# Windowed-attention kernel: loading the postponed half rows one row at a time, spread over regions

## The chip, the cores and the metric

The kernel runs on one core of one Trainium2 chip. The metric is the device time of one execution in microseconds. The median of three runs of the kernel before is 1763.54 us. All data are float32.

## What is computed

An image batch x of shape 8 x 56 x 56 x 256 goes through group normalization (32 groups) and a bi-level routing attention, and the result is added to x:

```python
q, k, v = split(conv1x1(groupnorm(x)))             # 256 channels each
a_r = mean_per_region(q) @ mean_per_region(k)      # 7 x 7 = 49 regions of 8 x 8 pixels
idx = top_k(a_r, 4)                                # each region takes the keys and values of 4 regions
o = softmax(q * 256**-0.5 @ k[idx]) @ v[idx]       # 8 heads of 32
out = x + conv1x1_out(o + depthwise3x3(v))         # the 3x3 part is called lepe
```

The four regions that a region attends to are known only at run time. So keys are gathered by GpSimd from SBUF, and values by DMA from DRAM.

## The kernel before, in words

**Tiling.** A "row" is one of the 56 rows of regions in the batch (7 per image): 8 pixel rows of 56 pixels, 448 positions, held as two channel halves of 128 partitions. One row of both halves is 448 KB, one half 224 KB. A region r is one of 392; row g holds regions 7g to 7g+6.

**Order of work.** Every engine has a hand-written instruction stream, a loop over steps s (0 to 56) and in it over the seven regions rc. In the turn of region r = 7s + rc, TensorE turns the first half of the softmax probabilities of r, computes the scores of r+1 (`scores`, L1098), attends region r-1 (`attend`, L1125), turns the other half, and does a slice of the projections. ScalarE does the exponentials and empties PSUM banks, VectorE the maxima, the scaling and the 3x3 taps (L737). There are three slots of gathered values, v_sel.

**SyncE's queue.** `select_values` (L322) issues four DMAs of 64 KB for each region, 256 KB in all, each for one of the chosen regions. In the turn of r it does so for r+2, once the slot is free, that is once region r-1 has been attended. `attend` waits for all four. This queue also stores the values of new rows (`store_values`, L301).

**GpSimd's queue.** In the turn of r it gathers the keys for r+2 (`gather_keys`, L382, waits for the scores of r), adds the attention output of r-2 to the lepe row (`take_region`, L393), and then does what the turn has by its number: `mid_tap` in 1 and 2, `halo` in 3 or 6, `normalize` in 4 and 5, the residual load `load_resid` (L449, L451) in 5, the store of the previous row `store_row` (L456, L459) in 6. It runs about a region ahead of TensorE, since its waits are for earlier regions. Its DMAs have a queue of their own; an issue holds the engine for over half a microsecond.

**Postponed rows.** For 25 rows (`LATE`) the second half (output channels 128 to 255) of the output projection isn't done in the row's own step. Instead, `spill_row` (L463) writes the finished lepe row to DRAM, and the last steps, from TAIL = 49 on, do the projection, since nothing else is left to project there. `LATE_GROUPS` are nine groups of two or three rows; `LATE_AT` gives group 0 to step 49, 1 to 50 and so on to 4 at step 53, then groups 5 and 6 (five rows) to step 54, and 7 and 8 (five rows) to step 55. `late_rows(s)` is the list of the step's rows. TensorE projects the first three in turns 0, 1 and 2 of the step (`project_late`, L1038), the fourth and fifth in turns 5 and 6; VectorE then adds bias and x (`late_half`, L835).

Their inputs come through GpSimd's queue. `load_late` (L477) brings a group of spilled rows into slots of xn: two DMAs (one per channel half) of 672 KB for three rows, 448 KB for two. It is called in turn 4 of the step before for each group of the step. It waits until the rows' slots are free (for the first three groups, until the q projections of the rows there before are done; later, until the group three before has been projected), and until all 25 spills have landed. `load_late_x` (L485) brings the second half of x for a group in one DMA (672 or 448 KB), in turn 6 of the step before, into the space of k_all that is no longer used. It waits until the last even image's keys have been gathered, or until the store of the group three before is done. `store_late` (L490) stores a group in one DMA, in turn 3 of its own step, the second group of a step in turn 1 of the next. There are three sets of three slots; each set has one semaphore for the rows and one for x.

```python
LATE_GROUPS = ((5, 12, 19), (26, 33, 40), (6, 13, 20), (27, 34, 41), (8, 15, 22), (29, 36, 43), (10, 17),
               (24, 31, 38), (45, 47))
LATE_AT = {TAIL: (0,), TAIL + 1: (1,), TAIL + 2: (2,), TAIL + 3: (3,), TAIL + 4: (4,), TAIL + 5: (5, 6),
           TAIL + 6: (7, 8)}
```

Of the kernel before, what the change touches and what calls it, by code (L numbers as in the profile page):

```python
# [20 lines left out]
KC = C // P  # L21
# [17 lines left out]
X_RING = 2 * NWIN  # L39
# [4 lines left out]
ROWS = NB * NWIN  # L44
# [11 lines left out]
LATE = [g for group in LATE_GROUPS for g in group]  # L56
LATE_AT = {TAIL: (0,), TAIL + 1: (1,), TAIL + 2: (2,), TAIL + 3: (3,), TAIL + 4: (4,), TAIL + 5: (5, 6),
           TAIL + 6: (7, 8)}
LATE_SETS = 3
LATE_SLOTS = 3  # L60
# [22 lines left out]
def late_rows(s):  # L83
    return [g for i in LATE_AT.get(s, ()) for g in LATE_GROUPS[i]]
# [51 lines left out]
def attention_kernel(nc, x, w_qkv, w_out, b_qkv, b_out, w_tap, b_tap, ident_d, group_d, v_dram, spill, out):  # L136
    place, early_chunks = chunk_places()

    with ExitStack() as ctx:
# [3 lines left out]
        def sem(name):  # L143
            return ctx.enter_context(nc.semaphore(name))
# [58 lines left out]
        resid_in = [sem(f"resid_in{i}") for i in range(2)]  # L203
        out_stored = [sem(f"out_stored{i}") for i in range(2)]
        spilled = sem("spilled")
        late_in = [sem(f"late_in{i}") for i in range(LATE_SETS)]
        late_x_in = [sem(f"late_x_in{i}") for i in range(LATE_SETS)]
        late_stored = [sem(f"late_stored{i}") for i in range(LATE_SETS)]

        chunk_full = [sem(f"chunk_full{i}") for i in range(EARLY_BANKS)]  # L210
# [24 lines left out]
        def late_set(i):  # L235
            first = LATE_SLOTS * (i % LATE_SETS)
            return slice(first, first + len(LATE_GROUPS[i]))

        def late_place(g):
            i = next(i for i, group in enumerate(LATE_GROUPS) if g in group)  # L240
            return i, LATE_SLOTS * (i % LATE_SETS) + LATE_GROUPS[i].index(g)

        def late_dram(rows, i):
            group = LATE_GROUPS[i]
            return rows[group[0]:group[-1] + 1:group[1] - group[0], :, 1, :].rearrange("i p r -> p i r")
# [9 lines left out]
        def wait_full(eng, kind, n, k):  # L255
            i, before = place[kind, n, k]
            eng.wait_ge(chunk_full[i], before + 1)
# [109 lines left out]
        def _(pool):  # L367
# [94 lines left out]
                pool.wait_ge(o_row_done, NWIN * (g + 1))  # L462
                pool.dma_start(spill[LATE.index(g)], lepe[:, :, g % LEPE_RING, :]).then_inc(spilled, 16)  # L463

            def load_late(i):
                group = LATE_GROUPS[i]
                if i < LATE_SETS:
                    for j in range(len(group)):
                        wait_full(pool, "q", ROWS - X_RING + LATE_SLOTS * i + j, 0)
                        wait_full(pool, "q", ROWS - X_RING + LATE_SLOTS * i + j, 1)  # L470
                else:
                    for g in LATE_GROUPS[i - LATE_SETS]:
                        wait_full(pool, "late", g, 1)
                pool.wait_ge(spilled, 16 * len(LATE))
                at = LATE.index(group[0])
                for k in range(KC):
                    pool.dma_start(xn[:, k, late_set(i), :], spill[at:at + len(group), :, k, :].rearrange(  # L477
                        "i p r -> p i r")).then_inc(late_in[i % LATE_SETS], 16)

            def load_late_x(i):  # L480
                if i < LATE_SETS:
                    pool.wait_ge(k_sel_done, NREG * (NB - 1))
                else:
                    pool.wait_ge(late_stored[i % LATE_SETS], 16 * (i // LATE_SETS))
                pool.dma_start(late_x[:, late_set(i), :], late_dram(x, i)).then_inc(late_x_in[i % LATE_SETS], 16)  # L485

            def store_late(i):
                for g in LATE_GROUPS[i]:
# [22 lines left out]
            for s in range(STEPS):  # L511
                rr, kv, xr = s % NWIN, s + KV_LEAD, s + STAT_LEAD
                for rc in range(NWIN):
                    r = s * NWIN + rc
                    if is_region(r + 2):
                        gather_keys(r + 2)
                    if is_region(r - 2):
                        take_region(r - 2)

                    if rc == 0 and is_row(s + LOAD_LEAD):  # L520
                        load_x(s + LOAD_LEAD)
                    elif rc == 1 and is_row(s + MID_LEAD):
                        mid_tap(s + MID_LEAD, 0)
                    elif rc == 2:
                        if is_row(s + MID_LEAD):
                            mid_tap(s + MID_LEAD, 1)
                        if s - 1 in LATE:
                            spill_row(s - 1)
                    elif rc == 3:
                        if rr == LAST and is_row(xr):  # L530
                            image_rstd(xr // NWIN)
                        if rr and is_row(kv):
                            halo(kv)
                    elif rc == 4 and is_row(s + NORM_LEAD):
                        normalize(s + NORM_LEAD, 1)
                    elif rc == 5:
                        if is_row(s + NORM_LEAD):
                            normalize(s + NORM_LEAD, 0)
                        if is_row(s):
                            load_resid(s)  # L540
                    elif rc == 6:
                        if is_row(s - 1):
                            store_row(s - 1)
                        if rr == 0 and is_row(kv):
                            halo(kv)

                    if rc == 1:
                        for i in LATE_AT.get(s - 1, ())[1:]:
                            store_late(i)
                    elif rc == 3:  # L550
                        for i in LATE_AT.get(s, ())[:1]:
                            store_late(i)
                    elif rc == 4:
                        for i in LATE_AT.get(s + 1, ()):
                            load_late(i)
                    elif rc == 6:
                        for i in LATE_AT.get(s + 1, ()):
                            load_late_x(i)

        @block.scalar  # L560
        def _(act):
# [150 lines left out]
        def _(dve):  # L712
# [117 lines left out]

            def late_half(g):
                i, j = late_place(g)
                dve.wait_ge(late_x_in[i % LATE_SETS], 16 * (i // LATE_SETS + 1))
                wait_full(dve, "late", g, 1)
                dve.scalar_tensor_tensor(late_x[:, j, :], bank_of("late", g, 1)[:, 0:ROW], bout[:, 1:2],  # L835
                                         late_x[:, j, :], ALU.add, ALU.add).then_inc(free("late", g, 1), 1)
# [158 lines left out]
        def _(pe):  # L995
# [34 lines left out]
            def project_late(g, first, last):  # L1030
                place_i, slot = late_place(g)
                for i in range(first, last):
                    half, part = divmod(i, KC)
                    cols = slice(HALF * half, HALF * (half + 1))
                    if i == 0:
                        pe.wait_ge(late_in[place_i % LATE_SETS], 16 * KC * (place_i // LATE_SETS + 1))
                        wait_bank(pe, "late", g, 1)
                    ins = pe.matmul(bank_of("late", g, 1)[:, cols], wout[:, part, P:2 * P], xn[:, part, slot, cols],  # L1038
                                    start=(part == 0), stop=(part == KC - 1))
                if last == QUARTERS:  # L1040
                    ins.then_inc(full("late", g, 1), 1)
# [301 lines left out]
```

## Time and profile before

| | |
|---|---|
| median of 3 runs | 1763.54 us (1760.93 to 1764.39) |
| the profiled execution's own time | 1764.58 us |
| its span, first to last instruction | 1762.8 us |
| granted TensorE clock, mean | 0.993 |
| TensorE busy | 1697.1 us (96%) |
| VectorE busy | 1527.3 us (87%) |
| ScalarE busy | 1463.7 us (83%) |
| GpSimd busy | 1151.4 us (65%) |
| SyncE's DMA queue | 129.71 MB |
| GpSimd's DMA queue | 100.02 MB |

How to read the rows: times are microseconds of one execution, from the start of the span. PE is TensorE's matmuls, PEld its weight loads, DVE VectorE, ACT ScalarE, POOL GpSimd, SP SyncE. Granted clock 1.00 is 2.4 GHz, 0.50 is 1.2 GHz. DMA share is the mean busy share of the core's 16 DMA engines; it can be a little over 1 in a short window. The tail, from which most rows are taken, lasts from about 1541 us to the end.

### The profile page before, as it was taken

The numbers are of one execution on the slowest core, as the hardware profiler recorded it, in microseconds if no ns is written. First come the engines' busy times: TensorE is split into PE (matmuls) and PEld (weight loads), VectorE is DVE, ScalarE is ACT, GpSimd is POOL, SyncE is SP. The second block draws the span as 40 slices with busy tenths as digits, with TensorE's granted clock in tenths as the row PEclk, the third lists the DMA queues.
The fourth block names the chain that finished last, engine by engine and source line by source line (L and its number), as shares of the span: only waits on it lengthen the run. The fifth ranks groups of instructions, "written<-read, shape, count | busy, mean of one in ns | idle before, by whom it ended". The sixth has DMA issues, their size and how long they took to land.

```text
span 1762.8 us, 76270 instructions
## 1 busy us (share of the span) xinstructions
PE 1697.1 (96%) x26568; PEld 1371.2 (78%) x26568; DVE 1527.3 (87%) x3329; ACT 1463.7 (83%) x4793; POOL 1151.4 (65%) x2525
## 2 busy tenths in 40 slices
PE   4999999999999999999999999999999999999987
PEld 4878887877778778778778778787787787777765
DVE  6478989899898899988898989988998888899984
ACT  1488888888888888888888888888888888878764
POOL 3256666677666776776766776667666666666762
PEclk9999999999999999999999999999999999999998
DMA  5323434343434443444443444434433333556563
GB/s 186 90 83 111 146 108 142 111 145 118 133 121 128 123 142 119 128 127 125 126 133 120 134 129 118 134 117 134 131 119 109 114 107 113 156 176 222 174 235 136
DMA packets 163945, 234.61 MB, mean 133 GB/s; under 512 B 18864, under 2 KB 146240, under 8 KB 163568
## 3 DMA queue, kind: packets, MB, share of 16 engines
q1 hardware_dynamic: 141408, 129.71, 25.1%
q0 software_dynamic: 22160, 100.02, 17.0%
q8 instruction: 219, 3.59, 0.9%
q14 instruction: 158, 1.29, 0.2%
HBM read 166.80 MB, written 62.85 MB: 130 GB/s over the span
## 4 chain that ended last, share of the span: by engine, by line
PE 64%; ACT 17%; DVE 11%; issue 4%; DMA 3%; POOL 0%; SPq 0%; POOLq 0%; ACTq 0%; DVEq 0%
PE chunk_bank L1011 18%; ACT probs L617 14%; PE pt_bank L1111 13%; PE s_bank L1098 12%; PE o_bank L1125 8%; DVE neg_max L840 6%; PE chunk_bank L1025 6%; DVE lepe L737 3%; PE chunk_bank L1053 2%; DMA v_sel<-v_dram 2%; ACT probs_t L624 2%; PE o_bank L1135 1%; PE s_bank L1011 1%; ACT v_stage L589 1%; PE chunk_bank L1073 1%
## 5 line engine op out<-in xcount | busy, mean ns | idle before, releaser
L617 ACT ACTIVATE probs<-s_bank,neg_max 128x256 f32<-128x256 f32 x1568 | 739.4, 484 | 158.3 <-DVE neg_max L840 157.7
L840 DVE TENSOR_REDUCE neg_max<-s_bank 128x2 f32<-128x512 f32 x784 | 506.1, 686 | 134.5 <-PE s_bank L1098 133.2
L737 DVE SCALAR_TENSOR_TENSOR lepe<-v_band,taps,lepe 128x448 f32<-128x448 f32 x896 | 611.1, 728 | 0.0
L382 POOL COPY k_sel<-k_all 128x128 f32 x1568 | 408.9, 305 | 290.9 <-PE s_bank L1098 277.2
L1011 PE MATMUL chunk_bank<-xn,wqkv 128*128 128x224 f32 x2544 | 570.6, 356 | 2.5 <-DVE xn L773 2.5
L624 ACT COPY probs_t<-pt_bank 128x512 f32<-128x512 f32 x784 | 467.3, 596 | 69.9 <-PE pt_bank L1111 68.9
L1111 PE MATMUL pt_bank<-ident,probs 128*128 128x128 f32 x3136 | 494.0, 280 | 0.2
L1011 PEld LDWEIGHTS chunk_bank<-xn,wqkv 128*128 128x128 f32 x2544 | 442.4, 192 | 9.3 <-DVE xn L773 2.6
L1111 PEld LDWEIGHTS pt_bank<-ident,probs 128*128 128x128 f32 x3136 | 359.7, 141 | 53.4 <-ACT probs_t L624 0.9
L393 POOL TENSOR_TENSOR lepe<-o_norm,lepe 128x128 f32<-128x128 f32 x392 | 251.2, 641 | 165.5 <-DVE o_norm L858 164.2
L617 ACT ACTIVATION_READ_ACCUMULATOR probs<-s_bank,neg_max 128x1 f32 x1568 | 332.2, 212 | 0.0
L1125 PEld LDWEIGHTS o_bank<-probs_t,v_sel 128*32 128x32 f32 x12544 | 193.8, 110 | 160.3 <-issue 149.0
L1098 PE MATMUL s_bank<-k_sel,q_all 32*64 32x256 f32 x6272 | 270.6, 400 | 18.9 <-ACT probs L617 6.9
L1125 PE MATMUL o_bank<-probs_t,v_sel 128*32 128x64 f32 x12544 | 257.4, 222 | 9.3 <-DMA v_sel<-v_dram 8.5
L1098 PEld LDWEIGHTS s_bank<-k_sel,q_all 32*64 32x64 f32 x6272 | 92.0, 130 | 93.6 <-ACT probs L617 57.3
L404 POOL TENSOR_SCALAR lepe<-v_band,taps,btap 128x448 f32<-128x448 f32 x112 | 162.2, 1448 | 0.0
L1025 PE MATMUL chunk_bank<-lepe,wout 128*128 128x224 f32 x696 | 151.0, 353 | 1.0 <-POOL lepe L393 1.0
L442 POOL TENSOR_SCALAR xn<-xn,rstd,shift 128x448 f32<-128x448 f32 x96 | 123.1, 1282 | 12.3 <-DVE shift_sum L801 12.3
L1025 PEld LDWEIGHTS chunk_bank<-lepe,wout 128*128 128x128 f32 x696 | 123.5, 190 | 2.3 <-POOL lepe L393 1.2
L851 DVE COPY recips<-rdenom 128x128 f32<-128x128 f32 x392 | 108.5, 277 | 13.4
L858 DVE TENSOR_TENSOR o_norm<-o_bank,recips_t 128x128 f32<-128x128 f32 x392 | 110.1, 281 | 6.7 <-PE o_bank L1125 6.7
L628 ACT COPY recips_t<-o_bank 128x128 f32<-128x128 f32 x392 | 113.9, 291 | 0.7 <-PE o_bank L1135 0.7
(77 smaller groups left out, 1299.5 us busy)
## 6 DMA issues: line engine op xcount, KB each, us to landing
v_sel<-v_dram SPq DMA_DIRECT2D x1568, 64.0 KB
xn<-x_dram POOLq DMA_DIRECT2D x56, 448.0 KB, 5.0
v_dram<-v_stage SPq DMA_DIRECT2D x112, 224.0 KB
resid<-x_dram POOLq DMA_DIRECT2D x31, 448.0 KB, 4.2
out_dram<-resid POOLq DMA_DIRECT2D x31, 448.0 KB
spill<-lepe POOLq DMA_DIRECT2D x25, 448.0 KB, 3.6
xn<-spill POOLq DMA_DIRECT2D x14, 672.0 KB, 6.7
resid<-x_dram POOLq DMA_DIRECT2D x25, 224.0 KB, 3.4
```

Source lines behind the costliest of these rows:

```text
L382: last = pool.tensor_copy(k_sel[:, r % K_SLOTS, :, RT * j:RT * (j + 1)], k_all[:, b % 2, :, bass.ds(reg[j] * RT, RT)])
L393: pool.tensor_tensor(cells, o_norm[:, r % 2, :].rearrange("p (k r c) -> p k r c", k=KC, r=RS), cells, ALU.add).then_inc(o_row_done, 1)
L404: pool.tensor_scalar(in_image(lepe[:, k, n % LEPE_RING, :]), v_band[:, n % BANDS, k, 1:1 + RS, 1:1 + W], taps[:, k, MID_TAP:MID_TAP + 1], ...
L617: act.activation(probs[:, u, :], s_bank[:, u, 0:KEYS], ACT.Exp, bias=neg_max[:, r % 2, u:u + 1], accum_out=denom[:, r % 2, u:u + 1]).then_ ...
L624: act.copy(probs_t[:, r % 2, hf, :], pt_bank[:, :]).then_inc(probs_t_evac, 1)
L737: ins = dve.scalar_tensor_tensor(row, v_band[:, n % BANDS, k, t // 3:t // 3 + RS, t % 3:t % 3 + W], taps[:, k, t:t + 1], row, ALU.mult, AL ...
L840: dve.tensor_reduce(neg_max[:, r % 2, 2 * hf:2 * hf + 2], s_bank[:, 2 * hf:2 * hf + 2, 0:KEYS], AX.X, ALU.max, negate=True).then_inc(max_d ...
L1011: ins = pe.matmul(bank_of(kind, n, k)[:, cols], wqkv[:, part, col:col + P], xn[:, part, n % X_RING, cols], start=(part == 0), stop=(part = ...
L1025: ins = pe.matmul(bank_of("out", g, m)[:, cols], wout[:, part, P * m:P * (m + 1)], lepe[:, part, g % LEPE_RING, cols], start=(part == 0), ...
L1098: last = pe.matmul(s_bank[RT * k:RT * (k + 1), u, 0:KEYS], q_all[s, g % Q_RING, k, rc, :], k_sel[s, r % K_SLOTS, k, :], start=True, stop=True)
L1111: t = pe.transpose(pt_bank[:, at:at + P], probs[:, u, P * c:P * (c + 1)], ident[:])
L1125: last = pe.matmul(o_bank[HD * u:HD * (u + 1), RT * k:RT * (k + 1)], v_sel[:, r % V_SLOTS, c, HD * head:HD * (head + 1)], probs_t[:, r % 2 ...
```

## The change

The two loading functions now take a row g in place of a group i, and each slot has its own semaphore for rows and for x, nine of each in place of three. `load_late(g)` issues one DMA of 448 KB for both channel halves; it waits only for its own slot, or for the group three before as until now, and only for the spills up to its own row. `load_late_x(g)` issues one DMA of 224 KB. In the step before, the first three rows are loaded in turns 3, 4 and 5, one each, and their x in turn 6. Where a step has five rows (54 and 55), the fourth and fifth are loaded in turns 0 and 1 of the step itself, each with its x right behind it. The stores of groups stay as they are. The rest is the waits of the readers, `late_half` and `project_late`.

```diff
--- before.py
+++ after.py
@@ -203,8 +203,8 @@
         resid_in = [sem(f"resid_in{i}") for i in range(2)]
         out_stored = [sem(f"out_stored{i}") for i in range(2)]
         spilled = sem("spilled")
-        late_in = [sem(f"late_in{i}") for i in range(LATE_SETS)]
-        late_x_in = [sem(f"late_x_in{i}") for i in range(LATE_SETS)]
+        late_in = [sem(f"late_in{i}") for i in range(LATE_SETS * LATE_SLOTS)]
+        late_x_in = [sem(f"late_x_in{i}") for i in range(LATE_SETS * LATE_SLOTS)]
         late_stored = [sem(f"late_stored{i}") for i in range(LATE_SETS)]
 
         chunk_full = [sem(f"chunk_full{i}") for i in range(EARLY_BANKS)]
@@ -462,27 +462,24 @@
                 pool.wait_ge(o_row_done, NWIN * (g + 1))
                 pool.dma_start(spill[LATE.index(g)], lepe[:, :, g % LEPE_RING, :]).then_inc(spilled, 16)
 
-            def load_late(i):
-                group = LATE_GROUPS[i]
+            def load_late(g):
+                i, slot = late_place(g)
                 if i < LATE_SETS:
-                    for j in range(len(group)):
-                        wait_full(pool, "q", ROWS - X_RING + LATE_SLOTS * i + j, 0)
-                        wait_full(pool, "q", ROWS - X_RING + LATE_SLOTS * i + j, 1)
+                    wait_full(pool, "q", ROWS - X_RING + slot, 0)
+                    wait_full(pool, "q", ROWS - X_RING + slot, 1)
                 else:
-                    for g in LATE_GROUPS[i - LATE_SETS]:
-                        wait_full(pool, "late", g, 1)
-                pool.wait_ge(spilled, 16 * len(LATE))
-                at = LATE.index(group[0])
-                for k in range(KC):
-                    pool.dma_start(xn[:, k, late_set(i), :], spill[at:at + len(group), :, k, :].rearrange(
-                        "i p r -> p i r")).then_inc(late_in[i % LATE_SETS], 16)
-
-            def load_late_x(i):
+                    for before in LATE_GROUPS[i - LATE_SETS]:
+                        wait_full(pool, "late", before, 1)
+                pool.wait_ge(spilled, 16 * (sorted(LATE).index(g) + 1))
+                pool.dma_start(xn[:, :, slot, :], spill[LATE.index(g)]).then_inc(late_in[slot], 16)
+
+            def load_late_x(g):
+                i, slot = late_place(g)
                 if i < LATE_SETS:
                     pool.wait_ge(k_sel_done, NREG * (NB - 1))
                 else:
                     pool.wait_ge(late_stored[i % LATE_SETS], 16 * (i // LATE_SETS))
-                pool.dma_start(late_x[:, late_set(i), :], late_dram(x, i)).then_inc(late_x_in[i % LATE_SETS], 16)
+                pool.dma_start(late_x[:, slot, :], x[g, :, 1, :]).then_inc(late_x_in[slot], 16)
 
             def store_late(i):
                 for g in LATE_GROUPS[i]:
@@ -550,12 +547,15 @@
                     elif rc == 3:
                         for i in LATE_AT.get(s, ())[:1]:
                             store_late(i)
-                    elif rc == 4:
-                        for i in LATE_AT.get(s + 1, ()):
-                            load_late(i)
+
+                    if rc >= 3 and late_rows(s + 1)[rc - 3:rc - 2] and rc < 6:
+                        load_late(late_rows(s + 1)[rc - 3])
                     elif rc == 6:
-                        for i in LATE_AT.get(s + 1, ()):
-                            load_late_x(i)
+                        for g in late_rows(s + 1)[:3]:
+                            load_late_x(g)
+                    elif rc < 2 and late_rows(s)[rc + 3:rc + 4]:
+                        load_late(late_rows(s)[rc + 3])
+                        load_late_x(late_rows(s)[rc + 3])
 
         @block.scalar
         def _(act):
@@ -830,7 +830,7 @@
 
             def late_half(g):
                 i, j = late_place(g)
-                dve.wait_ge(late_x_in[i % LATE_SETS], 16 * (i // LATE_SETS + 1))
+                dve.wait_ge(late_x_in[j], 16 * (i // LATE_SETS + 1))
                 wait_full(dve, "late", g, 1)
                 dve.scalar_tensor_tensor(late_x[:, j, :], bank_of("late", g, 1)[:, 0:ROW], bout[:, 1:2],
                                          late_x[:, j, :], ALU.add, ALU.add).then_inc(free("late", g, 1), 1)
@@ -1033,7 +1033,7 @@
                     half, part = divmod(i, KC)
                     cols = slice(HALF * half, HALF * (half + 1))
                     if i == 0:
-                        pe.wait_ge(late_in[place_i % LATE_SETS], 16 * KC * (place_i // LATE_SETS + 1))
+                        pe.wait_ge(late_in[slot], 16 * (place_i // LATE_SETS + 1))
                         wait_bank(pe, "late", g, 1)
                     ins = pe.matmul(bank_of("late", g, 1)[:, cols], wout[:, part, P:2 * P], xn[:, part, slot, cols],
                                     start=(part == 0), stop=(part == KC - 1))
```

## Rows read from the trace of the kernel before

**Rows 1.** The page, busy tenths in 40 slices of the span.
```profile
PE   4999999999999999999999999999999999999987
...
DMA  5323434343434443444443444434433333556563
```

**Rows 2.** Windows, L1098 alone: length, busy (x instructions), PEclk, DMA share, GB/s.
```profile
1545.00:1550.30 5.30, 0.69 (x16) 0.24 (x16) 1.00 0.39 125
1550.30:1683.50 133.20, 22.81 (x528) 7.81 (x528) 1.00 0.63 203
1683.50:1694.30 10.80, 0.69 (x16) 0.24 (x16) 0.68 0.55 196
1694.30:1718.70 24.40, 4.14 (x96) 1.42 (x96) 1.00 0.63 207
1718.70:1728.20 9.50, 0.69 (x16) 0.24 (x16) 0.64 0.69 248
1728.20:1744.20 16.00, 2.76 (x64) 0.94 (x64) 1.00 0.32 102
```

**Rows 3.** Timeline of weight loads: start, us, instructions, [idle before <- its end].
```profile
1546.57 0.49 PEld L1125 LDWEIGHTS o_bank<-probs_t,v_sel 128*32 128x32 f32 x32 [1.28 <-DMA v_sel<-v_dram]
...
1683.59 0.24 PEld L1098 LDWEIGHTS s_bank<-k_sel,q_all 32*64 32x64 f32 x16 [0.30 <-ACT probs L617]
1688.58 0.84 PEld L1125 LDWEIGHTS o_bank<-probs_t,v_sel 128*32 128x32 f32 x32 [4.75 <-DMA v_sel<-v_dram]
...
1694.38 0.23 PEld L1098 LDWEIGHTS s_bank<-k_sel,q_all 32*64 32x64 f32 x16 [0.17 <-issue]
...
1722.20 0.84 PEld L1125 LDWEIGHTS o_bank<-probs_t,v_sel 128*32 128x32 f32 x32 [3.20 <-DMA v_sel<-v_dram]
```

**Rows 4.** All instructions that read v_sel, whole span: waits (us, times).
```profile
  PEld o_bank L1125: 10.7, 5
```

**Rows 5.** The chain that ended last, 1676 to 1700: start, us, what.
```profile
1675.69 12.85 DMA v_sel<-v_dram
```

**Rows 6.** Timeline of POOL, steps 48 and 53.
```profile
1540.14 1.72 POOL L382 COPY k_sel<-k_all 128x128 f32 x4
...
1671.72 2.98 POOL L477 DMA_DIRECT2D xn<-spill  x4
...
1676.35 0.57 POOL L451 DMA_DIRECT2D resid<-x_dram  x1
...
1678.74 0.58 POOL L459 DMA_DIRECT2D out_dram<-resid  x1
1679.31 1.49 POOL L485 DMA_DIRECT2D k_all<-x_dram  x2
1680.80 0.99 POOL L382 COPY k_sel<-k_all 128x128 f32 x4
```

**Rows 7.** Windows, all engines: PE, PEld, DVE, ACT, POOL, PEclk, DMA share, GB/s.
```profile
1671.00:1687.00 16.00, 13.02 (x216) 9.65 (x214) 14.17 (x30) 12.49 (x45) 12.56 (x28) 1.00 0.92 317
1679.00:1683.00 4.00, 3.93 (x67) 3.04 (x66) 3.79 (x9) 3.60 (x15) 3.62 (x8) 1.00 1.05 356
1691.00:1695.00 4.00, 4.00 (x29) 2.98 (x28) 1.43 (x4) 2.03 (x7) 0.00 (x0) 0.62 0.25 77
```

**Rows 8.** DMA issues (KB, us to landing), then lines (duration ns min/median/max).
```profile
resid<-x_dram POOLq DMA_DIRECT2D x31, 448.0 KB, 4.2
...
xn<-spill POOLq DMA_DIRECT2D x14, 672.0 KB, 6.7
resid<-x_dram POOLq DMA_DIRECT2D x25, 224.0 KB, 3.4
...
L449 POOL DMA_DIRECT2D resid<-x_dram x25: 596/596/651, 264.1 to 1503.7; - x25
...
L463 POOL DMA_DIRECT2D spill<-lepe x25: 673/693/711, 280.3 to 1520.6; - x25
...
L477 POOL DMA_DIRECT2D xn<-spill x18: 724/767/798, 1527.8 to 1708.6; - x18
```

## The prediction, on record before the changed kernel ran

> **What bounds the kernel now.** I read four things in this order: the page's slices, the length of one region in the last part, the wait that ends late there, and what moved on the DMA engines meanwhile.
>
> The slices [rows 1] show TensorE at 9 tenths almost everywhere, so over most of the span the kernel is paced by the PE queue, which the change doesn't touch. What stands out is the end: the DMA row rises from 3 or 4 tenths to 5 and 6 in the last eight slices.
>
> Every region issues one group of 16 score matmuls (L1098), so counting them measures the pace [rows 2]. A region of the tail takes 4.00 us (64 matmuls in 16.0 us). From 1550.3 to 1683.5 there are 528, 33 regions in 133.2 us, which is 1.2 us over 33 x 4.00. But one region takes 10.8 us and another 9.5 us, at a mean granted clock of 0.68 and 0.64. They cost 6.8 and 5.5 us over 4.0, **12.3 us together**.
>
> Inside the first one [rows 3]: scores at 1683.59, then nothing until the attend matmuls (L1125) start at 1688.58, after 4.75 us of idle ended by the DMA into v_sel. From there the 32 weight loads take 0.84 us where they took 0.49 at 1546.57: behind the idle time TensorE runs at its 1.2 GHz level instead of 2.4 GHz, and the next scores come at 1694.38. The second region has 3.20 us of idle at 1722.20 and the same 0.84 us behind it. So each stall costs about twice its idle time in the first case (4.75 becomes 6.8) and 3.2 becomes 5.5 in the second. Over the whole execution the weight loads waited for v_sel five times, 10.7 us, and all five lie in the tail [rows 4]. There is also 1.3 us in a region of step 49 (5.3 us from 1545.0 to 1550.3 with 16 score matmuls [rows 2]), with a 1.28 us wait for v_sel in it [rows 3].
>
> Why v_sel is late: the chain of waits names one 64 KB transfer that was issued at 1675.69 and took 12.85 us [rows 5]. It was wanted at about 1684.0, 8.3 us after issue. Just before and after its issue POOL had put into its queue [rows 6] four loads of spilled rows (2240 KB, region 4 of step 53), a residual row (448 KB), a store (448 KB) and two loads of x for late rows (1120 KB). With 256 KB of values per region for four regions that is 5280 KB. The 16 us from 1671 to 1687 moved 317 GB/s, 5.07 MB or some 4950 KB, at a share around 1 in the middle [rows 7]. So the DMA engines were saturated by that burst, and the value gathers stood beside it. At 1718.7 the burst for step 55 does it again.
>
> **The change, part by part.** The bytes stay the same. For steps with three late rows, two loads of 672 KB at region 4 become three of 448 KB at regions 3, 4 and 5. For the two steps with five late rows (54 and 55), four loads at region 4 become three there and two in regions 0 and 1 of the step itself. The late x loads go from one of 672 KB at region 6 to three of 224 KB at region 6, and in the five-row steps the last two x rows follow their rows to regions 0 and 1.
>
> *Backlog.* I take 356 GB/s [rows 7] as what the engines can do: about 1390 KB in a 4.0 us region. Demand before for step 54, region 3 of step 53 onward (values 256 KB each; the residual row in region 5, the two stores in 3 and 6): 928, 2496, 704, 1824, 256, 256, 256 KB. After: 1376, 704, 1152, 1376, 928, 928, 256 KB. No region is above capacity, while before region 4 alone exceeded it by 1100 KB and region 6 again by 430. For a second comparison take three consecutive regions: after, the heaviest (5, 6, 0) hold 3456 KB; a three-row step before held 1600 + 704 + 1376 = 3680 KB in regions 4 to 6, and such steps ran with 1.2 us lost in 33 regions [rows 2]. So the five-row steps should now behave like three-row ones. I take both long stalls as gone: **-12.3 us**, idle and slow clock together, since the clock fell only behind the idle time.
>
> *Step 49.* Its 1.3 us comes from the burst of 1344 KB at region 4 of step 48. After, 896 KB are issued by then and 448 KB later, so the value stores and the first gather of the new image land earlier, but the later load joins the x loads. Bounds: 0 and 1.3 recovered; I take -0.7.
>
> *The small remainders.* 1.2 us in the 33 regions [rows 2] and 0.4 in the six between the stalls. The 0.4 is a region with three taps and a late row on VectorE, and stays. Of the 1.2 I take half, -0.5; bounds 0 and -1.2.
>
> *Issues on POOL.* Before, 18 loads and 9 x loads; after, 25 and 25. An issue of 448 KB holds POOL 0.69 us, one of 224 KB 0.60, the present ones 0.77 [rows 8] and 0.75 [rows 6]: 32.2 - 20.6 = 11.6 us more of POOL, in about 230 us. What hides it: key gathers (L382) for region r+2 wait only for the scores of r and are used two scores later. In the burst of step 53 the gather behind the two x loads ran from 1680.80 to 1681.79 [rows 6]; its scores would have come at 1687.6, one unstalled region after 1683.59 [rows 3], so it was 5.8 us early. At most three issues are added in one stretch (one at region 5, two at region 6), 2.1 us, and the slack is over 5. Without that cover each microsecond would land on scores: 11.6 us at most. In the first step of an image, 49, the gathers were already catching up: the third ended at 1541.86 [rows 6] for scores at 1545.0, 3.2 us of slack. I take 0; bounds 0 and +3. The queue of SP gets no new instruction.
>
> *Waits.* load_late drops the wait for all 25 spills (now only those up to its own row) and the waits for a whole group. Later positions reach buffers that were freed at least three regions before (the fourth and fifth rows of step 55 follow the late rows of step 54's regions 0 to 2 and their store at region 3). The rows have at least three regions, 12 us, between issue and use, against landings of 6.7 us with 672 KB [rows 8]. No new stall there: 0. The x rows now land one by one, so the first late row of a step isn't held for three. That is in the -0.7 above.
>
> Sum: -12.3 - 0.7 - 0.5 = **-13.5 us**. The profiled execution took 1764.58 us around a span of 1762.8; it would take 1751.1. The median of the three runs is 1763.54, 1.0 below it, so I predict **1750.0 us**.
>
> **The rivals.** (a) *One collision remains.* The x loads at region 6, the stores and the two displaced rows follow one another closely through regions 5 to 1, and a gather there meets them. For it: 1376 KB in region 6 is at capacity. Against it: the three-row comparison. It would keep about one stall of 5.5 to 6.8: some 1757 us.
>
> (b) *Nothing is gained*, because what delays the gathers is the total in the tail and not the burst, or the released load is only moved to the next regions. Then 1763.5. Against it: windows like 1691 to 1695, with a DMA share of 0.25 [rows 7], right behind the saturated ones, so there is room to move into. The Trainium skill (DMA: Bandwidth & Descriptors, Queues, rings and completion order) says each DMA engine goes round the queues it has work for, one packet at a time; by that rule a deep POOL queue could hold SP's small gathers back only by a share and not by its whole depth. The 12.85 us of a 64 KB transfer [rows 5] shows that the share is poor when the other queue stays full.
>
> (c) *Slower: the fixed cost of each transfer decides.* From 224 KB in 3.4 us and 448 KB in 4.2 us [rows 8], a transfer has 2.6 us that don't depend on size. If POOL's queue served its transfers one after the other, steps 54 and 55 would have four more each (10 for 6): 10.4 us per step in the queue that is already full, 20.8 in all, of which the idle DMA windows of a step might cover half. The stalls would stay and grow by 10.4: 1774 us. It decides once the fixed parts of a step's transfers no longer overlap. Against it: four loads issued within 3 us, with what followed, moved at 356 GB/s [rows 6, 7]. The Trainium skill (DMA: Bandwidth & Descriptors, Bandwidth) has a rule that speaks against the change: batch to 1 MiB or more, for transfers below it stay short of peak; its fit gives 2.0 us of fixed cost. No row here shows that cost serially.
>
> **How the numbers follow.** The forecast 0.74, (a) 0.13, (b) 0.07, (c) and anything like it on POOL 0.06. The range starts at 1747 (all 15.2 us of excess recovered gives 1748.3, and one run of before was 2.6 under the median) and goes to 1759, which takes in +3 for POOL and case (a). Less than 0.2% (3.5 us) can't be told from no change here. Faster 0.87, same 0.07, slower 0.06.
>
> **What would show it.** Right: no wait of L1125 for v_sel over 1 us after 1541; every region in 1683 to 1730 near 4.0 us at clock 1.00; no 4 us window at share 1 twice in a row in the tail; L382 still waiting for scores, with no score matmul behind POOL. Wrong: a 1.30 us group of weight loads anywhere in the tail, a region over 6 us, or L1098 waiting for L382.

## The result, and the profile after

| | before | changed |
|---|---|---|
| median, first series | 1763.34 us (4 runs) | 1753.09 us (4 runs, 1751.71 to 1755.16) |
| ratio | | 0.9946, 95% interval 0.9933 to 0.9959 |
| profiled execution | 1764.58 us | 1755.16 us |
| span | 1762.8 us | 1753.4 us |
| granted clock, mean | 0.993 | 0.996 |

The change made the kernel 10.3 us faster. A second series of six runs gave 1752.51 us against 1764.13, ratio 0.9942 (0.9925 to 0.996). One execution each of e7 and e10 below took 2741 and 2740 us, at a mean granted clock of 0.62 and 0.56, and their medians and all ratios leave it out. The forecast of 1750.0 is 3.1 us below the first median, inside the range.

Three traces are read below with one yardstick: the time from the 50th last group of scores (L1098) to the last, 49 intervals, the last image. The scores of consecutive regions lie 3.99 or 4.00 us apart where nothing stands in the way, which makes 196. The kernel before took **211.2 us** for it, the changed one **200.9** in its first profile and **197.4** in a second one (e12 below). The image before it took 206.2 in the kernel before and 206.1 and 206.2 in the other two.

In the 40 slices of the page, beside [rows 1], the DMA row ends in 34466574 tenths, where it ended in 33556563: about as high as before, for the bytes haven't changed. Windows of the changed kernel with L1098 alone, as in [rows 2] (length, PE busy and count, PEld busy and count, clock, DMA share, GB/s):

```profile
1547.90:1683.80 135.90, 23.51 (x544) 8.05 (x544) 1.00 0.65 206
1683.80:1691.30 7.50, 0.69 (x16) 0.24 (x16) 0.77 0.62 197
1691.30:1716.90 25.60, 4.14 (x96) 1.42 (x96) 1.00 0.70 223
1716.90:1732.90 16.00, 2.77 (x64) 0.95 (x64) 1.00 0.60 198
```

34 regions in 135.9 us: the losses ahead of step 54 are gone. Of the two long regions one is left, 7.5 us at a mean clock of 0.77, in step 54; the one of step 55 is gone. The six regions behind it took 25.6 us, 1.6 over 24: two of them 4.4 us each, and one, in turn 4 of step 54, 4.8 us. In that one two 3x3 taps on VectorE took 2.56 us, where the next pair took 1.47:

```profile
1697.57 2.56 DVE L737 SCALAR_TENSOR_TENSOR lepe<-v_band,taps,lepe 128x448 f32<-128x448 f32 x2
1702.38 1.47 DVE L737 SCALAR_TENSOR_TENSOR lepe<-v_band,taps,lepe 128x448 f32<-128x448 f32 x2
```

The timeline of the weight loads (start, us; idle before), beside [rows 3]:

```profile
1683.85 0.24 PEld L1098 LDWEIGHTS s_bank<-k_sel,q_all 32*64 32x64 f32 x16 [0.30 <-ACT probs L617]
1686.54 0.83 PEld L1125 LDWEIGHTS o_bank<-probs_t,v_sel 128*32 128x32 f32 x32 [2.44 <-DMA v_sel<-v_dram]
1691.38 0.23 PEld L1098 LDWEIGHTS s_bank<-k_sel,q_all 32*64 32x64 f32 x16 [0.17 <-issue]
```

It is the same kind of stall as before, 2.44 us of idle in place of 4.75, and again the lower clock level behind it: 0.83 us for 32 weight loads that take 0.49. The transfer it waited for, from the chain of waits, beside [rows 5]:

```profile
1677.43 9.06 DMA v_sel<-v_dram
```

9.06 us in place of 12.85. And all that reads v_sel, beside [rows 4] (us of waiting, times):

```profile
  PEld o_bank L1125: 2.8, 2
```

GpSimd's issues, beside [rows 8] (count, duration in ns min/median/max):

```profile
L474 POOL DMA_DIRECT2D xn<-spill x25: 704/724/753, 1523.4 to 1716.6; - x25
...
L482 POOL DMA_DIRECT2D k_all<-x_dram x25: 537/539/567, 1538.0 to 1717.4; - x25
```

That is 31.6 us of issues where there were 20.5. No score matmul in the tail waited for a key gather. The waits of GpSimd's gathers and of the scores' weight loads, 1500 to 1753 (us, times, longest):

```profile
POOL k_sel L382 <- PE s_bank L1098: 30.9, 26, 5.4
PEld s_bank L1098 <- ACT probs L617: 15.9, 52, 0.4
```

**Where the values stood.** The view that I hadn't split by queue in the prediction is the one that explains most. For each 4.0 us window, the packets, MB and share of the 16 engines of GpSimd's queue (q0) and SyncE's queue (q1), which in this stretch carries the value gathers. They need 0.26 MB a region. The kernel before, 1675.7 to 1679.7:

```profile
q0 software_dynamic: 312, 1.44, 97.1%
q1 hardware_dynamic: 62, 0.06, 4.8%
```

and 1679.7 to 1683.7:

```profile
q0 software_dynamic: 259, 1.25, 89.4%
q1 hardware_dynamic: 141, 0.13, 10.2%
```

The changed kernel, 1673.6 to 1677.6:

```profile
q0 software_dynamic: 227, 1.15, 82.1%
q1 hardware_dynamic: 182, 0.16, 13.3%
```

and 1677.6 to 1681.6:

```profile
q0 software_dynamic: 249, 0.98, 72.7%
q1 hardware_dynamic: 214, 0.20, 15.6%
```

So the values can fall behind while the engines move less than the 356 GB/s that the prediction took as their capacity: the two windows after hold 1.31 and 1.18 MB, against 1.42, and the two queues together 95% and 88% of the engines' time. In these four windows SyncE's queue got less than it needs: 0.06 and 0.13 MB before, 0.16 and 0.20 after. After, it is still short, only less so. But the shortfall alone doesn't tell whether a stall comes. In the four windows from the start of the burst this execution has 0.11, 0.30, 0.16 and 0.20 MB, and e12, the same kernel without the stall, has 0.10, 0.30, 0.20 and 0.15.

### The profile page after: what moved, and what is told of

Its sections match the earlier page's. It is cut to its first block, busy times and chain, and to the rows that moved or that the text cites. A ratio compares the mean times of both kernels' runs of the same rounds, so it can differ in the third digit from the quotient of the medians.

```text
span 1753.4 us, 76313 instructions
## 1 busy us (share of the span) xinstructions
PE 1692.8 (97%) x26568; PEld 1368.0 (78%) x26568; DVE 1524.4 (87%) x3329; ACT 1460.4 (83%) x4793; POOL 1155.3 (66%) x2548
## 4 chain that ended last, share of the span: by engine, by line
PE 64%; ACT 18%; DVE 12%; issue 4%; DMA 1%; SPq 0%; POOL 0%; POOLq 0%; ACTq 0%; DVEq 0%
PE chunk_bank L1011 17%; ACT probs L617 14%; PE pt_bank L1111 13%; PE s_bank L1098 13%; PE o_bank L1125 8%; DVE neg_max L840 6%; PE chunk_bank L1025 6%; DVE lepe L737 4%; PE chunk_bank L1053 2%; ACT probs_t L624 2%; PE o_bank L1135 1%; PE s_bank L1011 1%; ACT v_stage L589 1%; PE chunk_bank L1073 1%; ACT q_all L598 1%
## 5 line engine op out<-in xcount | busy, mean ns | idle before, releaser
L1098 PE MATMUL s_bank<-k_sel,q_all 32*64 32x256 f32 x6272 | 270.6, 400 | 18.3 <-ACT probs L617 4.5
L1098 PEld LDWEIGHTS s_bank<-k_sel,q_all 32*64 32x64 f32 x6272 | 92.0, 130 | 93.1 <-ACT probs L617 57.1
L442 POOL TENSOR_SCALAR xn<-xn,rstd,shift 128x448 f32<-128x448 f32 x96 | 122.1, 1272 | 12.3 <-DVE shift_sum L801 12.3
L1135 PE MATMUL o_bank<-ident,recips 128*128 128x128 f32 x392 | 108.2, 276 | 4.6 <-DVE o_norm L858 3.6
```

The costliest lines, as they stand in the source:

```text
L1098: last = pe.matmul(s_bank[RT * k:RT * (k + 1), u, 0:KEYS], q_all[s, g % Q_RING, k, rc, :], k_sel[s, r % K_SLOTS, k, :], start=True, stop=True)
```

## The experiments

All are variants of the changed kernel unless said. "Last image" is the yardstick above (49 intervals; the expectation of e9 calls them 48 regions), in the variant's one profile; "waits" are those of the attend weight loads for v_sel in that execution. The intervals reach some 3 us to either side, so apart from e10 the medians don't tell the variants from each other, and one profile isn't enough either: the changed kernel itself read 200.9 and 197.4. In the diffs `...` marks lines left out.

| run | median us | ratio to before (95%) | last image us | waits for v_sel us, times |
|---|---|---|---|---|
| changed, first | 1753.09 | 0.9946 (0.9933 to 0.9959) | 200.9 | 2.8, 2 |
| e1 rows, one turn | 1756.74 | 0.9961 (0.9944 to 0.9979) | 202.2 | 7.2, 5 |
| e2 only five-row steps | 1752.39 | 0.9933 (0.9912 to 0.9954) | 199.4 | 0.8, 2 |
| e3 groups, spread | 1753.96 | 0.9946 (0.9925 to 0.9968) | 198.6 | 3.0, 4 |
| e4 rows in halves | 1752.43 | 0.9935 (0.9915 to 0.9956) | 198.7 | 0.6, 1 |
| e5 displaced later | 1753.53 | 0.9939 (0.9919 to 0.9958) | 197.5 | 1.6, 2 |
| e6 register load split | 1754.48 | 0.9943 (0.9924 to 0.9963) | 202.8 | 5.4, 6 |
| e7 both | 1753.89 | 0.9943 (0.9928 to 0.9957) | 201.9 | 3.8, 2 |
| e8 four rows not loaded | 1750.81 | 0.9924 (0.9902 to 0.9945) | 197.4 | 0.8, 1 |
| e9 halves, one turn | 1754.24 | 0.9949 (0.993 to 0.9969) | 201.4 | 3.4, 3 |
| e10 x by row alone | 1764.25 | 0.9999 (0.9986 to 1.0013) | 211.1 | 10.7, 6 |
| e11 later, in halves | 1752.37 | 0.9939 (0.9923 to 0.9956) | 198.4 | 0.8, 2 |
| e12 changed, again | 1752.51 | 0.9942 (0.9925 to 0.996) | 197.4 | 2.5, 4 |

**e1: the same transfers, at the old moments.**

```diff
-                    if rc >= 3 and late_rows(s + 1)[rc - 3:rc - 2] and rc < 6:
-                        load_late(late_rows(s + 1)[rc - 3])
+                    if rc == 4:
+                        for g in late_rows(s + 1):
+                            load_late(g)
...
-                        for g in late_rows(s + 1)[:3]:
+                        for g in late_rows(s + 1):
                             load_late_x(g)
-                    elif rc < 2 and late_rows(s)[rc + 3:rc + 4]:
-                        load_late(late_rows(s)[rc + 3])
-                        load_late_x(late_rows(s)[rc + 3])
```

> The same 25 and 25 transfers as the changed kernel, but all rows of a step are issued in turn 4 of the step before and all x in turn 6, as the groups were. Theory A, that the moments of the loads decide: the two long stalls of the kernel before return, and the time is 1762 to 1766 us. Theory B, that the size of a transfer decides (single rows mix better with the value gathers than groups of three): it stays at 1751 to 1755 us. Theory C, that each transfer has a serial fixed cost or that its issue on GpSimd shows: it is slower than the kernel before, above 1768 us.

Neither of the first two. 1756.7 us: 7.5 us below the kernel before (3.7 to 9.9 by the ratio's interval), so more than half of the gain is there, as the medians have it, although nothing is spread. The two stalls are still at steps 54 and 55, with 2.40 and 2.33 us of idle (before: 4.75 and 3.20), and the clock didn't fall behind them. Weight loads of e1, the first of the two:

```profile
1683.88 0.49 PEld L1123 LDWEIGHTS o_bank<-probs_t,v_sel 128*32 128x32 f32 x32 [2.40 <-DMA v_sel<-v_dram]
1687.11 0.23 PEld L1096 LDWEIGHTS s_bank<-k_sel,q_all 32*64 32x64 f32 x16 [0.17 <-issue]
```

So this stall costs 1.9 us where one with 2.44 us of idle and the lower clock cost the changed kernel 3.5. Theory C is out: 23 more transfers, with ten in place of six in the bursts for steps 54 and 55, made nothing slower. The edit changes more than the size: a row's transfer takes both channel halves of one row, where a group's took one half of two or three rows.

**e2: spreading only for the two five-row steps.**

```diff
-                    if rc >= 3 and late_rows(s + 1)[rc - 3:rc - 2] and rc < 6:
+                    if s + 1 < TAIL + 5:
+                        if rc == 4:
+                            for g in late_rows(s + 1):
+                                load_late(g)
+                    elif rc >= 3 and late_rows(s + 1)[rc - 3:rc - 2] and rc < 6:
...
-                    elif rc == 6:
+                    if rc == 6:
```

> Rows for steps 49 to 53 are issued in turn 4 all at once, those for steps 54 and 55 as in the changed kernel. If the gain comes from the two five-row steps alone: 1753 to 1756 us, with at most 1.5 us more than the changed kernel, in the regions behind the bursts of steps 48 to 52. If spreading the three-row steps is worth something of its own: above 1756.

1752.4 us: as good as the changed kernel. In its profile 2.1 us are lost in four single regions of steps 49 to 52, where e12 lost 0.8. What spreading the three-row steps is worth can't be told from nothing here; the gain that shows is in the steps with five rows.

**e3: the kernel before, with its groups at spread moments.**

```diff
-                    elif rc == 4:
-                        for i in LATE_AT.get(s + 1, ()):
-                            load_late(i)
-                    elif rc == 6:
-                        for i in LATE_AT.get(s + 1, ()):
-                            load_late_x(i)
+                    if rc in (3, 5):
+                        for i in LATE_AT.get(s + 1, ())[:1]:
+                            load_late(i, (rc - 3) // 2)
+                    elif rc == 6:
+                        for i in LATE_AT.get(s + 1, ())[:1]:
+                            load_late_x(i)
+                    elif rc < 2:
+                        for i in LATE_AT.get(s, ())[1:]:
+                            load_late(i, rc)
+                            if rc:
+                                load_late_x(i)
...
```

`load_late` takes the channel half as its second argument and issues that one alone; the first three groups wait for 24 of the 25 spills.

> The transfers of the kernel before (18 loads of groups and 9 of x) at spread moments: the two channel halves of the first group in turns 3 and 5, those of the second group of steps 54 and 55 in turns 0 and 1 of the step itself, with its x in turn 1. Theory A (moments): 1751 to 1756 us, like the changed kernel. Theory B (size of the transfer): 1760 to 1765 us, like the one before.

1754.0 us, last image 198.6: theory A. With e1 this gives the main finding: **either half of the change, the moments or the single rows, brings most of the gain alone**, and the two don't add up. For the single rows that is 7.5 us of 10.3, with intervals of e1 and the changed kernel that overlap.

**e4: twice as many transfers of rows.**

```diff
-                pool.dma_start(xn[:, :, slot, :], spill[LATE.index(g)]).then_inc(late_in[slot], 16)
+                for k in range(KC):
+                    pool.dma_start(xn[:, k, slot, :], spill[LATE.index(g), :, k, :]).then_inc(late_in[slot], 16)
...
```

TensorE's wait for a row counts both transfers.

> The changed kernel with each row load made as two transfers of 224 KB: 25 transfers and some 15 us of GpSimd's issue time more, the same bytes at the same moments. Theory A, issues and fixed costs hidden: within 1.5 us of the changed kernel, 1752 to 1755 us. Theory C, fixed cost of a transfer (2.6 us) or its issue time shows: 3 to 15 us slower than the changed kernel, with score matmuls that wait for the key gathers or a longer wait for v_sel.

Theory A again: 1752.4 us. GpSimd now issues for 40.5 us (27.2 + 13.3), 20 more than in the kernel before, and the median shows no time for it. Its profile isn't free of a trace of it, though: three regions took 4.45, 4.45 and 4.80 us, and beside them a pair of taps on VectorE took 2.20, 2.20 and 2.55 us, while GpSimd was issuing and copying keys. No pair took so long in the last image of the kernel before or of e1 and e9, which issue at the old moments. Whether GpSimd's work at these moments slows the taps wasn't tested.

**e5: the fourth and fifth rows in turns 1 and 2.**

```diff
-                    elif rc < 2 and late_rows(s)[rc + 3:rc + 4]:
-                        load_late(late_rows(s)[rc + 3])
-                        load_late_x(late_rows(s)[rc + 3])
+                    elif 1 <= rc < 3 and late_rows(s)[rc + 2:rc + 3]:
+                        load_late(late_rows(s)[rc + 2])
+                        load_late_x(late_rows(s)[rc + 2])
```

> The changed kernel with the fourth and fifth rows of steps 54 and 55 (and their x) loaded in turns 1 and 2 instead of 0 and 1. Its one remaining stall is at the attend of the step's first region in turn 1 of step 54 (2.44 us idle, 3.5 us in all), while the displaced loads of turns 0 and 1 are under way. If those loads hold the values back: the stall is gone or under 1 us and the time is 2 to 4 us below the changed kernel. If it is the short lead of that region's gathers (behind SyncE's register load of 2.2 us) with the transfers of turns 5 and 6: the stall stays at 2 us or more and the time is within 1 us.

No stall in its profile, last image 197.5, but the median is that of the changed kernel. What I took for a cure was chance: e12 shows the unedited kernel without the stall too, and e7 has these moments and the stall.

**e6: SyncE reads its region numbers in three portions.**

```diff
 GROUPS = {0: NWIN}
+SP_GROUPS = {0: 2, 2: 3, 5: 2}
...
-                if r % NWIN in GROUPS:
-                    value_regions.update(chosen(mybir.EngineType.SP, r, GROUPS[r % NWIN]))
+                if r % NWIN in SP_GROUPS:
+                    value_regions.update(chosen(mybir.EngineType.SP, r, SP_GROUPS[r % NWIN]))
```

> The changed kernel with SyncE's register load of 28 region numbers per step (2.2 us, right ahead of the gathers for the step's first region) split into three of 8, 12 and 8. If the short lead of that region's gathers makes the remaining stall: they are issued 1 us or more earlier, the stall of 2.44 us shrinks by as much, and the time falls by 1 to 3 us. If the load of the DMA engines alone makes it: no shift of the stall, time within 1 us, or slightly slower by the additional register loads.

No gain, 1754.5. The stall came in this profile too, with 2.72 us of idle, and the transfer at its end took 10.05 us. It had been issued 7.4 us before it was wanted, in the changed kernel 6.7 us before, so the lead grew by 0.7 us and the stall didn't shrink. A portion isn't cheap: the load of 8 or 12 numbers took 1.07 us, the one of all 28 took 2.17 (medians of 14 and of 4 of SyncE's register loads from 1600 us on, in e6 and in the changed kernel).

**e7: e5 and e6 together** (both diffs).

> Both of the above together. If each takes away its own part, there is no wait for v_sel over 0.5 us in the tail and the time is 1748 to 1751 us: the changed kernel less 3.5 us. If one is the whole cause, this is the same as that one alone.

It missed: 1753.9 us, with a wait of 3.17 us one region ahead of that place, in a region of 8.3 us. Neither edit takes the stall away for certain.

**e8: the fourth and fifth rows aren't loaded.** It bounds what moving them can give.

```diff
-                    elif rc < 2 and late_rows(s)[rc + 3:rc + 4]:
-                        load_late(late_rows(s)[rc + 3])
-                        load_late_x(late_rows(s)[rc + 3])
...
```

The waits for these four rows and their x are left out too, so their part of the output is not computed from the right data.

> The changed kernel without the loads of the fourth and fifth rows of steps 54 and 55 at all (rows 10, 17, 45 and 47; their second output half is computed from what lies in the slots), so 2688 KB less. It bounds what any other moment for these loads can give: if they make the remaining stall, it is gone, 1749 to 1751 us; if the stall stays at 2 us or more, it is made by the rest, the loads of turns 5 and 6 and the short lead.

1750.8 us, as the first case said: at most some 2 us are left in the moments of these four rows. There is no stall in its profile, but e12 has none either, with the four rows loaded.

**e9: transfers of 224 KB, all at the old moments** (the diffs of e1 and e4).

> Every row of a step in turn 4 of the step before and every x in turn 6, as in the kernel before, but with transfers of 224 KB throughout (two for each row). The row-by-row kernel at these moments had two stalls with 2.40 and 2.33 us of idle where groups of 672 KB had 4.75 and 3.20. If the size of the transfers sets how long the value gathers are held up: less than 1.5 us of idle at each place, the last image's 48 regions in 197.5 to 200.5 us (202.2 with 448 KB, 211.2 with 672 KB), the time 1752 to 1755. If what was gained there came from something else than size: the stalls stay at 2 us and the time is 1756 or more.

Between the cases: 1754.2 us, idle for v_sel 1.16 us at step 55 and none at step 54, but the last image took 201.4, above what I gave, with losses of 1.6 us in a region of step 54 and 1.3 in one of step 49 among others. The 1.6 us came another way: VectorE waited for the x of a late row, whose transfer, issued at 1679.29, took 6.93 us, and the exponentials and TensorE waited behind it.

```profile
1686.24 0.68 DVE L834 SCALAR_TENSOR_TENSOR k_all<-chunk_bank,bout,k_all 128x448 f32<-128x448 f32 x1 [1.54 <-DMA k_all<-x_dram]
```

What SyncE's queue got, region by region from the start of the burst (first four windows of 4.0 us): 0.26, 0.06, 0.13, 0.12 MB in the kernel before; 0.21, 0.10, 0.14, 0.14 in e10 (below), with the rows still in groups; 0.22, 0.10, 0.15, 0.16 in e1 with single rows; 0.22, 0.15, 0.21, 0.26 here. Only e9 stands out clearly, and it isn't a matter of size alone: its ten issues of rows hold GpSimd for 5.35 us, where the four before took 2.98, and its x loads begin 11.0 us after the first row's, 7.6 in the kernel before and 8.6 in e1.

**e10: the kernel before with only the x loads by row.**

```diff
-                pool.dma_start(late_x[:, late_set(i), :], late_dram(x, i)).then_inc(late_x_in[i % LATE_SETS], 16)
+                for g in LATE_GROUPS[i]:
+                    slot = late_place(g)[1]
+                    pool.dma_start(late_x[:, slot, :], x[g, :, 1, :]).then_inc(late_x_in[slot], 16)
...
```

> The kernel before with only the x loads made row by row (224 KB instead of 672 or 448 KB), still all in turn 6; the spilled rows stay in groups in turn 4. If the x loads, the last to be queued ahead of the late gathers, hold them up by their size: a good part of the two long stalls goes, 1756 to 1760 us. If the large transfers of spilled rows do it, within 2 us of the kernel before.

Nothing: 1764.3, last image 211.1, waits of 3.45 and 3.79 us at the two places. The size of the x loads isn't what holds the values back. e1 differs from this mainly in the loads of spilled rows, which come first in the burst, so the gain of e1 is put down to them.

**e11: e4 and e5 together, the candidate for something better.**

> The changed kernel with both edits that left no stall in their profiles: displaced rows in turns 1 and 2, and each row in two transfers of 224 KB. The last image should take 197.5 to 199 us with no wait for v_sel over 1.3 us; the time 1751 to 1753.5 us. Since each edit alone gave 1752.4 and 1753.5, I expect no clear gain over the changed kernel: at most 2 us.

1752.4 us, as expected no measurable gain over the changed kernel.

**e12: the changed kernel once more.**

> The changed kernel once more, unedited, to see whether the stall of its first profile (2.44 us idle at the first region of step 54, 3.5 us in all) is in every execution. If it is: last image 200.5 to 201.5 us, 1752 to 1755 us. If it comes and goes: last image near 198 us.

It comes and goes. Its windows with L1098 alone:

```profile
1549.50:1705.30 155.80, 26.96 (x624) 9.23 (x624) 1.00 0.66 208
1705.30:1714.10 8.80, 1.38 (x32) 0.47 (x32) 1.00 0.89 287
1714.10:1730.10 16.00, 2.77 (x64) 0.95 (x64) 1.00 0.62 205
```

39 regions of steps 49 to 54 in 155.8 us, without a loss; ahead of them 0.8 us are lost in step 49. What remains are two regions of 4.4 us right behind turns 5 and 6 of step 54, in which VectorE has three taps and a late row. In the kernel before, the second of them had lain inside the long stall.

## Why the prediction was right, point by point

**The two long stalls, -12.3 us.** Right in that the bursts make them, too large by what sometimes stays. In the first profile 3.5 us of stall are left and the second region of 4.4 us comes out (0.4): -8.4. In e12: -11.9. The step that was off is the one on backlog: "No region is above capacity", hence both gone. The capacity of the engines wasn't the measure. At 82% and 73% of the engines' time GpSimd's queue still left SyncE's only 0.16 and 0.20 MB of the 0.26 it needed, and one gather in the first profile took 9.06 us where it had been issued some 7 us ahead. And e1 keeps region 4 at 2496 KB, far over the 1390 KB of the backlog, yet is 7.5 us faster than the kernel before: by the account of backlog alone, single rows at unchanged moments gain nothing. In e12 the usual gaps of 0.39 and 0.38 us ahead of two attends of step 54 ended with a landing in v_sel, so there the margin is about nothing. That fits a stall that shows in three of the eight profiles with single rows spread over turns (the changed kernel, e6, e7) and not in the others (e2, e4, e5, e11, e12). What decides it in a given execution is open. The reading that the first stall costs "about twice its idle time" was too high too: 6.8 for 4.75 is 1.4 times, 5.5 for 3.20 is 1.7 times. The sum doesn't use it.

**Step 49, -0.7.** The 1.3 us there are gone in the first profile and 0.8 us are back in e12: -1.3 and -0.5, within the bounds given.

**Small remainders, -0.5.** All of the 1.2 us went, the upper bound.

**Not in the sum.** In the three executions with the stall, the region in turn 4 of step 54 is 0.8 us too long, with the slow pair of taps shown above (e4 and e11, without a stall, have such a region in step 53); the first profile's sum is then -8.4 - 1.3 - 1.2 + 0.8 = -10.1, against 211.2 - 200.9 = 10.3 read. For e12 it is -11.9 - 0.5 - 1.2 = -13.6, against 13.8. So the forecast of -13.5 describes the last image of an execution without the stall. The whole of that execution took 1752.35 us, 12.2 below the profiled one before, since the time outside its last image was 1.6 us longer. That the median came within 3.1 us of the forecast rests in part on how often the stall stays away, which the prediction didn't foresee.

**GpSimd, 0.** Right as far as the scores go: 11.1 us more of issues (11.6 forecast), and 20 more in e4, and no score matmul waited for them. Two errors partly cancel in the 11.6: the rows' issues took 18.1 us for 17.3, those of x 13.5 for 15.0. The slow taps of the first profile and of e4 may be a price that the prediction didn't consider; that wasn't tested.

**Its own signs.** By what it named as signs of being wrong, the first profile shows two: a region of 7.5 us, over 6, and a group of weight loads of 1.30 us at 1688.23, at the lower clock level. The third, scores that wait for key gathers, doesn't show. The 2.44 us of that profile also fail its first sign of being right, no wait for v_sel over 1 us. e12 has none of the wrong signs, but a wait of 1.32 us in step 49.

**The rivals.** (a), one collision remains, is what the first profile shows, at the place named and at half the price (3.5 us for 5.5 to 6.8). (b) falls with the result, and with e1 and e3. (c) falls with e4 and e1: transfers were added at no cost that the medians show, and splitting the groups into rows (e1) helped. The batching rule of the Trainium skill (DMA: Bandwidth & Descriptors, Bandwidth) thus didn't decide here: it is about the throughput of one stream, and what counts here is how long another queue waits. The rule of the Trainium skill that each engine goes round its queues one packet at a time (Queues, rings and completion order) agrees in that the values always got something. The records count 312 packets of one queue to 62 of the other in the worst window, so it was no even turn-taking. Smaller row transfers were faster at unchanged turns (e1). That they raise the share of the other queue shows only in e9, where the moments moved as well; e1's shares are about those of e10, which gained nothing. So what makes e1 faster is open.

## What to carry to other kernels

When a small gather with a fixed lead shares the DMA engines with bulk loads of another queue, look at MB per queue in windows of one turn, not only at the total share. The gather can fall short while the engines move less than they can. Such windows show the exposure, and don't foretell the stall. Spread the bulk loads, or cut them into smaller transfers; either was worth most of it here, and both are cheap where the issuing engine has slack. The stretch that an edit touches is a finer yardstick than the whole time, but take more than one profile: the unedited changed kernel read 200.9 and 197.4 us, and a single profile made e5 look like a cure.

## What was not expected

Cutting transfers at unchanged moments (e1) brought 7.5 us: groups of 672 and 448 KB against single rows of 448.

The time outside the last image varies by 5.2 us between these profiles, more than the 3.5 us of the stall that comes and goes. The span less the last image was 1551.6 us before, 1552.5 in the changed kernel, 1553.2 in e12, 1550.1 in e9 and 1555.3 in e6. Part of it is the start: the first scores stand at 86.4 us in e9 and at 88.8 in e11.

After 2.40 us of idle the next matmuls ran at full clock (e1), after 2.44 us at the lower level (changed kernel), so nearly equal stalls cost 1.9 and 3.5 us. In e7 the 32 weight loads behind 3.17 us of idle took 0.49 us, at full clock, and the level fell only then: the mean granted clock was 0.62 from 1684 to 1686 us and 0.52 from 1686 to 1688, and the stall cost 4.3 us.
